# Sixteen-head attention: value products in two groups of six key tiles, and heads packed through memory into one block

## The reference, cut to what matters

```
x1 = layernorm(x)
qh, kh, vh = split(x1 @ Wq.T + bq), split(ctx @ Wk.T + bk), split(ctx @ Wv.T + bv)     # 16 heads of 8
attn = softmax(mask(qh @ kh.T / sqrt(8)))                                              # 56 x 1500 per head
x = x + concat_heads(attn @ vh) @ Wo.T + bo
```

## Time and profile before

| | us |
|---|---|
| median of 3 runs | 3760.95 (3756.37 to 3769.27) |
| the profiled execution | 3759.2 |
| its span | 3757.5 |
| stage L1a, start of its first to its last scores product | 392.8 to 1194.5 |
| stage L2a, the same | 1431.9 to 2231.7 |
| one batch of either in the middle | 25.3 |

### The profile page before, as it was taken

How to read it: one execution, slowest core, us unless ns; L and a number is a source line. 1 busy time by engine, 2 the same in 40 slices (tenths; PEclk the granted TensorE clock), 3 DMA queues, 4 the chain that set the end, 5 groups by cost and what they waited for, 6 DMA issues and landing times. The chain is left out here.

```text
span 3757.5 us, 96452 instructions
## 1 busy us (share of the span) xinstructions
PE 3297.9 (88%) x40550; PEld 2418.8 (64%) x40550; DVE 2546.4 (68%) x3627; ACT 2068.1 (55%) x3846; POOL 1158.9 (31%) x1140
## 2 busy tenths in 40 slices
PE   7676899999998669999999993689999999999989
PEld 4465677777776556777777762456666666666655
DVE  5744677777774447777777746588878787878851
ACT  3321566666564124666656544467676767677733
POOL 0024222212211442222222200145454555555530
PEclk8887999999999788999999996799999999999989
DMA  7954565566562335544554510100000000000000
GB/s 220 267 140 137 155 172 152 155 168 164 143 168 53 99 111 137 137 118 123 138 123 118 137 33 0 32 25 17 25 17 25 24 19 25 17 25 17 17 16 12
DMA packets 136406, 345.99 MB, mean 92 GB/s; under 512 B 56515, under 2 KB 78603, under 8 KB 135979
## 3 DMA queue, kind: packets, MB, share of 16 engines
q1 hardware_dynamic: 132843, 333.40, 33.7%
q0 software_dynamic: 3136, 6.46, 0.5%
HBM read 174.68 MB, written 17.17 MB: 51 GB/s over the span
## 5 line engine op out<-in xcount | busy, mean ns | idle before, releaser
L2115 POOL TENSOR_TENSOR l_S<-l_S,l_shift 125x448 f32<-125x448 f32 (+1 forms) x416 | 461.2, 1151 | 319.9 <-ACT l_shift L2347 317.4
L1431 ACT ACTIVATE L1a_probs<-ps 125x448 f32<-125x448 f32 x768 | 382.7, 545 | 205.7 <-PE ps L1331 192.3
L1431 ACT ACTIVATE L2a_probs<-ps 125x448 f32<-125x448 f32 x768 | 382.8, 544 | 204.9 <-PE ps L1331 191.3
L1464 DVE TENSOR_REDUCE L2a_chunk_max<-ps 112x1 f32<-112x1000 f32 x256 | 301.2, 1197 | 151.0 <-PE ps L1290 150.6
L1464 DVE TENSOR_REDUCE L1a_chunk_max<-ps 112x1 f32<-112x1000 f32 x256 | 301.1, 1196 | 138.5 <-PE ps L1290 138.1
L2328 ACT ACTIVATE ctx_stats<-ps 125x512 f32<-125x512 f32 (+1 forms) x416 | 247.9, 596 | 179.6 <-PE ps L2173 170.4
L2225 PE MATMUL ps<-l_S,l_z 125*128 125x448 f32 x768 | 342.5, 542 | 0.0
L2392 DVE TENSOR_REDUCE l_norms<-ctx_stats 125x8 f32<-125x512 f32 (+1 forms) x416 | 268.3, 676 | 76.9 <-ACT ctx_stats L2328 76.8
L1290 PE MATMUL ps<-L2a_keys,L2a_queries 96*112 96x500 f32 x768 | 264.1, 426 | 47.3 <-DVE L2a_chunk_max L1464 20.3
L2418 DVE SCALAR_TENSOR_TENSOR l_S<-ps,l_neg_cols,l_inv_norms 125x448 f32<-125x448 f32 x384 | 255.4, 679 | 73.6 <-PE ps L2194 69.8
L1235 POOL TENSOR_TENSOR L1a_k_lo<-L1a_k_full,L1a_k_hi 128x1000 fp32r<-128x1000 f32 x64 | 115.0, 1797 | 616.0 <-ACT L1a_k_hi L1388 613.6
(11 more groups left out here) (491 smaller groups left out, 7030.8 us busy)
## 6 DMA issues: line engine op xcount, KB each, us to landing
L1a_keys<-L1a_k_hi SPq DMA_DIRECT2D x256, 187.5 KB
L2a_keys<-L2a_k_hi SPq DMA_DIRECT2D x256, 187.5 KB
a_ctx_T<-in_ctx_T SPq DMA_DIRECT2D x32, 750.0 KB, 12.1
L1a_ctx_T<-in_ctx_T SPq DMA_DIRECT2D x32, 750.0 KB, 6.2
xn<-L_valid SPq DMA_DIRECT2D x32, 750.0 KB, 7.7
L1a_keys<-L1a_k_lo SPq DMA_DIRECT2D x128, 187.5 KB
L2a_ctx_T<-in_ctx_T SPq DMA_DIRECT2D x32, 750.0 KB, 6.4
L2a_keys<-L2a_k_lo SPq DMA_DIRECT2D x128, 187.5 KB
```

The lines of the kernel that those rows point to most:

```text
L1431: nc.scalar.activation(probs[t % NPR][:, h * HQ // 2:(h + 1) * HQ // 2], s.ps[0:KP, i % 3, 0:HQ // 2], ACT.Exp).then_inc(probs_made, 1)
L1464: ins = nc.vector.tensor_reduce(chunk_max[:, n, 0:1], product, AX.XY, ALU.max)
L2115: nc.gpsimd.tensor_tensor(S[b % 2][0:r, t, :], S[b % 2][0:r, t, :], shift[0:r, :], ALU.add)\
```

## The change

- `GT` is 6 instead of 3: the value products come in two groups of six tiles (192 passes each), behind the scores of tile 7 and ahead of the next batch's scores. `NPR` is 10 instead of 6, and the buffers are counted on through the batches.
- The normalized heads go to one of two small tiles, `normed_heads`. SyncE stores each batch's four strips of 8 partitions to memory (`store_heads`), at the end of its turn for the next batch, and loads whole chunks back as one dense block of 128 rows (`load_heads`): three chunks during batches 11, 20 and 29, the rest at the end. `heads_out` is [128, 1792].
- The projection is one product a chunk instead of four, the bias product one instead of four; `wo` and `bv` are loaded dense, without the zeroing of `wo_quad`.
- Queries, their parts and the squares lie in the space of the probabilities; ACT waits once for the stores of the query terms before the batches, DVE no longer does.

```diff
--- before
+++ after
     def bias_product(self, pe):
-        for g in range(4):
-            mm = self.nc.tensor.matmul(self.s.ps[:, 7, 0:1], self.wo_quad[:, g, :], self.bv_quad[:, g:g + 1], start=(g == 0),
-                                       stop=(g == 3))
-        mm.then_inc(self.bias_made, 1)
+        self.nc.tensor.matmul(self.s.ps[:, 7, 0:1], self.wo[:, :], self.bv[:, :], start=True, stop=True)\
+            .then_inc(self.bias_made, 1)
...
-        for g in range(4):
-            mm = self.nc.tensor.matmul(self.s.ps[:, self.CHUNK_BANKS[c], 0:cols.stop - cols.start], self.wo_quad[:, g, :],
-                                       self.heads_out[:, g, cols], start=(g == 0), stop=(g == 3))
-        mm.then_inc(self.projected, 1)
+        self.nc.tensor.matmul(self.s.ps[:, self.CHUNK_BANKS[c], 0:cols.stop - cols.start], self.wo[:, :],
+                              self.heads_out[:, cols], start=True, stop=True).then_inc(self.projected, 1)
...
-    NQ, NKB, NPR, GT = 3, 3, 6, 3
+    NQ, NKB, NPR, GT = 3, 3, 10, 6
...
+    LOAD_AT = [-(-c * 4 * D // SQ) + 1 for c in (1, 2, 3)]
...
+        heads_dram = nc.dram_tensor(f"{layer}_heads", [4, DK, 4, TOK], F32, kind="Internal").ap()
...
-        probs = [sb(f"probs{n}", [KP, HQ]) for n in range(NPR)]
+        probs_space = sb("probs", [D, NPR, HQ])
+        probs = [probs_space[0:KP, n, :] for n in range(NPR)]
+        normed_heads = [sb(f"normed_heads{u}", [D, 4, SQ]) for u in range(2)]
...
-        q, q_hi, q_lo = heads_out[:, 0, :], heads_out[:, 1, :].bitcast(F32R), heads_out[:, 2, :].bitcast(F32R)
+        q, q_hi, q_lo, squares = (probs_space[:, 2 * n:2 * n + 2, :].rearrange("p n c -> p (n c)") for n in range(4))
+        q_hi, q_lo = q_hi.bitcast(F32R), q_lo.bitcast(F32R)
...
-            for j in range(4):
-                sp.dma_start(wo_quad[32 * j:32 * j + DK, :, :], a[f"{layer}_WoT"][j]).then_inc(quads_loaded, 16)
-                if biased:
-                    sp.dma_start(bv_quad[32 * j:32 * j + DK, :], a[f"{layer}_bv"][j]).then_inc(quads_loaded, 16)
+            sp.dma_start(wo[:, :], a[f"{layer}_WoT"].rearrange("j d c o -> (j d c) o")).then_inc(out_loaded, 16)
+            if biased:
+                sp.dma_start(bv[:, :], a[f"{layer}_bv"].rearrange("j d (c o) -> (j d c) o", o=1)).then_inc(out_loaded, 16)
...
-            nc.gpsimd.memset(wo_quad[:, :, :], 0.0).then_inc(zeroed, 1)
...
+            def store_heads(b):
+                sp.wait_ge(normed, b + 1)
+                for j in range(4):
+                    sp.dma_start(heads_dram[j, :, :, b * SQ:(b + 1) * SQ],
+                                 normed_heads[b % 2][32 * j:32 * j + DK, :, :]).then_inc(heads_stored[b % 2], 16)
+
+            def load_heads(first, last):
+                stored = -(-last // SQ)
+                sp.wait_ge(heads_stored[0], 64 * ((stored + 1) // 2))
+                sp.wait_ge(heads_stored[1], 64 * (stored // 2))
+                sp.dma_start(heads_out[:, first:last], heads_dram[:, :, :, first:last].rearrange("j d c q -> (j d c) q"))\
+                    .then_inc(heads_loaded, 16)
...
                 if b + 1 < B:
                     move_maxima(b + 1)
+                if b in LOAD_AT:
+                    load_heads(LOAD_AT.index(b) * 4 * D, (LOAD_AT.index(b) + 1) * 4 * D)
+                if b:
+                    store_heads(b - 1)
+            load_heads(12 * D, (B - 1) * SQ)
+            store_heads(B - 1)
+            load_heads((B - 1) * SQ, TOK)
+            sp.wait_ge(heads_loaded, 16 * 5)
...
-                                          probs[t % NPR][:, h * SQ:(h + 1) * SQ], start=(t == 0 and c == 0),
+                                          probs[(b * KT + t) % NPR][:, h * SQ:(h + 1) * SQ], start=(t == 0 and c == 0),
...
+            act.wait_ge(terms_stored, 96)
...
-                        nc.scalar.activation(probs[t % NPR][:, h * HQ // 2:(h + 1) * HQ // 2], s.ps[0:KP, i % 3, 0:HQ // 2],
-                                             ACT.Exp).then_inc(probs_made, 1)
+                        nc.scalar.activation(probs[(b * KT + t) % NPR][:, h * HQ // 2:(h + 1) * HQ // 2],
+                                             s.ps[0:KP, i % 3, 0:HQ // 2], ACT.Exp).then_inc(probs_made, 1)
...
-                if b == 0:
-                    dve.wait_ge(terms_stored, 96)
...
-                nc.vector.tensor_tensor(heads_out[:, :, b * SQ:(b + 1) * SQ], acc[:, :].rearrange("p (c q) -> p c q", c=4),
+                if b >= 2:
+                    dve.wait_ge(heads_stored[b % 2], 64 * (b // 2))
+                nc.vector.tensor_tensor(normed_heads[b % 2][:, :, :], acc[:, :].rearrange("p (c q) -> p c q", c=4),
...
-            (("heads_out", [D, 4, TOK]), ("wo_quad", [D, 4, D]), ("bv_quad", [D, 4]), ("out_bias", [D, 1])))
+            (("heads_out", [D, TOK]), ("wo", [D, D]), ("bv", [D, 1]), ("out_bias", [D, 1])))
```

More of the change, by code:

```diff
@@ L109, with __init__ @@
     CHUNK_BANKS = (5, 6, 7, 5)
-    def __init__(self, nc, s, stack, name, heads_out, wo_quad, bv_quad, bias):
+    def __init__(self, nc, s, stack, name, heads_out, wo, bv, bias):
         self.nc, self.s, self.stack = nc, s, stack
-        self.heads_out, self.wo_quad, self.bv_quad, self.bias = heads_out, wo_quad, bv_quad, bias
+        self.heads_out, self.wo, self.bv, self.bias = heads_out, wo, bv, bias
         self.sems = [stack.enter_context(nc.semaphore(f"{name}_{n}"))
@@ L1047, in sem @@
             return sems[-1]
-        heads_out, wo_quad, bv_quad, bias = s.heads_out, s.wo_quad, s.bv_quad, s.out_bias
+        heads_out, wo, bv, bias = s.heads_out, s.wo, s.bv, s.out_bias
         wq, wk, wv = sb("wq", [D, D]), sb("wk", [D, D]), sb("wv", [D, D])
@@ L1069, in attention_16_heads @@
         max_hi, max_lo = sb("max_hi", [RT, 2, RW], F32R), sb("max_lo", [RT, 2, RW], F32R)
-        probs = [sb(f"probs{n}", [KP, HQ]) for n in range(NPR)]
+        probs_space = sb("probs", [D, NPR, HQ])
+        probs = [probs_space[0:KP, n, :] for n in range(NPR)]
+        normed_heads = [sb(f"normed_heads{u}", [D, 4, SQ]) for u in range(2)]
         acc, inv = sb("acc", [D, 4 * SQ]), sb("inv", [D, 4 * SQ])
-        q, q_hi, q_lo = heads_out[:, 0, :], heads_out[:, 1, :].bitcast(F32R), heads_out[:, 2, :].bitcast(F32R)
+        q, q_hi, q_lo, squares = (probs_space[:, 2 * n:2 * n + 2, :].rearrange("p n c -> p (n c)") for n in range(4))
+        q_hi, q_lo = q_hi.bitcast(F32R), q_lo.bitcast(F32R)
         if masked:
-            mask_i, valid_all = k_full[0:B, :].bitcast(I32), heads_out[0:B, 3, 0:SK]
+            mask_i, valid_all = k_full[0:B, :].bitcast(I32), squares[0:B, 0:SK]
             neg_all = [k_hi[0:B, :], k_lo[0:B, :]]
@@ L1084, in attention_16_heads @@
             sem(n) for n in ("k_hi_made", "k_lo_made", "queries_made", "max_made", "hi_split", "row_moved", "scores_made"))
[L1085 to L1088, removed]
+        probs_made, probs_used, acc_taken, normed, heads_loaded = (
+            sem(n) for n in ("probs_made", "probs_used", "acc_taken", "normed", "heads_loaded"))
+        heads_stored = [sem(f"heads_stored{u}") for u in range(2)]
+        weights_loaded, mask_loaded, out_loaded, zeroed, cut, prep, q_product, q_made, q_split = (
+            sem(n) for n in ("weights_loaded", "mask_loaded", "out_loaded", "zeroed", "cut", "prep", "q_product",
                              "q_made", "q_split"))
@@ L1103, in load_first @@
                     .then_inc(ctx_loaded[b], 16)
-            sp.wait_ge(zeroed, 6)
+            sp.wait_ge(zeroed, 5)
             if biased:
@@ L1119, in set_first @@
             nc.gpsimd.memset(head_mask[:, :], 1.0).then_inc(zeroed, 1)
-            pool.wait_ge(zeroed, 6)
+            pool.wait_ge(zeroed, 5)
             nc.gpsimd.affine_select(out=head_mask[:, :], in_=head_mask[:, :], compare_op=ALU.is_ge, fill=0.0,
@@ L1134, in set_first @@
             nc.gpsimd.memset(keys[1][KQ:KS, :, :].bitcast(F32), 1.0).then_inc(ones_set, 1)
-        norm(on_sync=load_first, on_pool=set_first, squares=heads_out[:, 3, :])
+        norm(on_sync=load_first, on_pool=set_first, squares=squares)
         batches = ExitStack()
@@ L1541, in _ @@
             norm(("sums", B - 1, 0))
-            dve.wait_ge(quads_loaded, 16 * N_QUADS)
+            dve.wait_ge(out_loaded, 16 * N_OUT)
         batches.close()
         s.stale.append((sems, sem_stack))
-    return Projection(nc, s, ExitStack(), f"{layer}p", heads_out, wo_quad, bv_quad, bias[:, 0:1])
+    return Projection(nc, s, ExitStack(), f"{layer}p", heads_out, wo, bv, bias[:, 0:1])
 def quantized(nc, s, a, norm):
```

6 lines of the change are left out of this document (3 added, 3 removed).

## The result

On one chip, in turns: before 3758.69 us (3756.37 to 3769.27), after 3982.93 us (3979.9 to 3988.22). The ratio is **1.0595, 95% interval 1.0575 to 1.0614**: slower by 224 us. The forecast was 3940 us (3810 to 4005). The profiled execution took 3984.3 us, its span is 3982.6.

The account below looks back on a forecast made before the run. The prediction took TensorE (PE) to set the pace, busy 23.9 of 25.2 us a batch. Its terms, 2 - 7 + 166 + 34 - 19 + 10 - 0.5, less 4 us of existing stalls, gave +181: 3759 + 181 = 3940 us (3810 to 4005).

Parts of the forecast that it names:

- Part 2: Value groups of six in both 16-head stages: TensorE outruns its instruction fetch, 1.3 us a group, +166 us.
- the positions: Page starts relative to a group of six: 128 of 256 give 2.2 us stops, 57 sparse ones part of it.
- Rival 1: Groups of six: instruction fetch keeps up, groups run through, -15 us, 3744 us; chance 11%.
- rival 2: Groups of six: fetch counts from its packet only, 2.4 us; 0.5 us a group, 64 us, 3815 us; chance 10%.
- Part 3: 16-head stages: 38 full stalls each bring a half-clock stretch at 0.9 us, +34 us (0 to 77).
- Part 1: Batch schedule, four groups of three become two of six: +0.03 us a batch, +2 us (-36 to +12).
- first half of the batch: Part 1's step to the next scores behind the first group of six: gain 0.07 us, DVE's chain eats the rest.
- the second half: Part 1's step: second keys product waits for DVE's bank; second group ends at 723.15 against 723.10 before.
- The row of maxima: 16-head stages: the copy of the maxima leaves 0.7 us earlier, so its 14.7 us of waits shrink, -7 us (0 to -15).
- Part 4: Output projection behind each stage: lead of the next layer norm falls from 18.5 to 8.9 us, -19 us for both.
- Part 5: Heads through memory: 0 inside the stage (to +9), 4.9 us bare trip at each stage's end, +10 us for both.

Follow-up runs that it names:

- the twins: phase_few and phase_many: changed kernel with filler instructions making a batch 1024 instructions, differing only in fillers ahead of the first batch; 3929.71 and 4094.91 us.
- half: Changed kernel with each value product taking two heads' columns, so groups of six have 96 passes (half the values wrong); 3760.03 us, 1.0000 of the kernel before.
- run 256: Not a follow-up run and has no measured time: "run" is a verb here, PE executing 256 instructions, one 16 KB packet.
- gt3: Changed kernel with groups of three tiles instead of six, all else of the change kept; 3780.13 us, 1.0015 of the kernel before.
- before_gt2: Kernel before with groups of two tiles and nothing else of the change; 3746.07 us, 0.9939 of the kernel before.
- phase_many: Changed kernel, batches filled to 1024 instructions, 20 and 188 fillers ahead to put page boundaries where stops were long; 4094.91 us, 1.0861 of the kernel before.
- phase_few: Changed kernel, batches filled to 1024 instructions, 92 and 212 fillers ahead to put page boundaries where stops were fewest; 3929.71 us, 1.0410 of the kernel before.
- one_store: Changed kernel with groups of three and one 128-partition store of heads a batch instead of four small ones; 3761.42 us, 1.0005 of the kernel before.

## Why the prediction was right, and where it wasn't

- **Part 2, fetch stops**: +166 forecast; measured 159 us inside the groups and 11.5 just behind them, 1.3 us a group as forecast. Right in cause (the twins, half, the remainder 193) and in size. As many groups stop as the positions gave, 92 of 128 or 72%, like (128 + 57)/256, but not as reckoned: 57 of the 64 second groups and 35 of the 64 first. The size owes something to luck, errors that cancelled: most stops are shorter than 2.2 us (median 1.6), while L1a's first groups stop for 2.88 us in the mean behind the mask's transfers, which no term held. One reading of the mechanism was off: that PE, on entering a page, asks for the one after the next. PE goes on 2.2 to 3.0 us behind the start of the packet each time, so this packet brings the next page; the sum, which lets PE run 256 instructions and then wait, is as it should be. And PE stopped not twice in the stages before but in 10 groups. Rival 1 (the fetch keeps up) and rival 2 (64 us) are out. By the Trainium skill (Runtime: NRT & Kernel Launch, Instruction fetch mechanics) the fetch is hidden by the dispatch; this trace doesn't agree, with 159 us of stops in groups that take an instruction every 6.1 ns (2.34 us for 384).
- **Part 3, clock**: 38 slow stretches forecast at 0.9 us, 33 more came, at 1.3 us by the twins: 42 us against 34. Near in size, but the count was a choice that rested on one gap, and the row was misread: the gap of 1.62 us at 1004.54 is not the longest of the masked stage. This one is, and the clock stayed at 1.00 behind it:

```profile
1156.86 0.48 PE L1331 MATMUL ps<-L1a_queries,L1a_keys 100*125 100x224 f32 x2 [2.02 <-DMA L1a_queries<-L1a_max_lo]
```

- **Part 1, schedule**: the step that was mis-sized. +0.03 us a batch forecast, bounds up to +0.2; measured 25.82 against 25.31 us, some +31 us for both stages. The first half of the batch came out as followed through. In the second half, from the scores behind the first group to the product behind the second, 9.38 us were reckoned; it takes 9.63, and before it takes 9.01 in the median batch, where the sample batch of the earlier trace rows, which held the stop of the earlier trace rows, had 9.26. The second keys product, with no group beside it, waits for DVE's bank (17 us a stage at L1289), as part 1 said, but rows 0 behind it takes 0.93 us to the start of the group, where 0.55 was reckoned. The upper bound was too low.
- **The row of maxima**: -7 forecast; its waits (7.5 and 7.2 us) went wholly, but other waits stand before the same products, 5.4 us instead of 0.8, so -10. That nearly all of the 14.7 us were waits below a microsecond was misread: 8 of the 14 waits were longer, 11.1 us together.
- **Part 4, projection**: the lead 18.5 to 9.0 us in L1a and to 9.9 in L2a, against 8.9 forecast, -18 us. Right.
- **Part 5, trip**: 6.3 and 5.9 us at the two ends against 4.9. The four small stores hold SyncE's queue 0.69 us each (2.76 at 1343.54), where I took 0.31 to 0.33 from the loads of the earlier trace rows: the upper end of my own bound. Inside the stage 0 was right for six tiles, where other waits cover the late context, and +9 for three tiles (gt3).

Sum as measured, between the first and the last `sums` of each stage: +148 (stops in groups, 151.6 less 3.6), +12 (stops behind them), +42 (clock), +31 (schedule), -10 (maxima) and +3, a shift only, as 96 passes a stage that stood ahead of the first `sums` now stand behind it: +226 of +224.7. Outside it is +7 (stops in the first batches), -18, +12 and -3, so -2, where +0.5 was measured. That this closes so well is luck in part. Nor can the 11 us more of the beginning and the 13 less of the end be put down to the change: the first scores product comes at 392.8 us before and at 400.0 in before_gt2, with the same code up to there, and from the first L2258 to the end it is 1250.8 us before and 1236.95 in before_gt2 (1236.65 in the changed kernel). The forecast was 43 us low, 29 us of that the schedule and 8 the clock.

## What to carry to other kernels

Count instructions as well as columns: a run of small products that issues more than a page of 256 instructions in less than the time a page takes to come (here a page entered to the next one usable took 3.7 us in the median stop) stops the engine, whatever the data do; cut such runs, or make each product larger. The stop can also fall just behind the run, on a product that has no part in it. Before lengthening groups to save switches, look at who waits behind a group: here the best group was shorter than the one in use. And an engine that stands still now and then loses twice, as its clock follows.

## What the runs showed of the hardware that was not expected

- **When the packet starts.** A stop ends 2.2 to 3.0 us behind the start of its packet, in all 314 stops inside groups of three kernels (the changed one and the phase twins). But the packet starts between 0.0 and 10.2 us behind the page's first instruction (median 1.1 in the changed kernel). With the boundary between the first and the second group, 60 sparse instructions in 9 us, the packet often came only as the second group began: at 447.94 the page is entered, at 456.26 the packet starts, and the group from 456.19 on stops for 1.0 us. What asks for it so late is open.
- **Stops and clock.** Of the stops inside groups in the changed kernel, 1 of 48 under 1.6 us had a slow stretch at or within 5 us behind it, and 24 of 44 longer ones; in phase_many 10 of 47 and 34 of 76. In phase_few, with 99 stops of which 92 were under 1.6 us, 3 had one. Slow stretches came behind stops that fell just behind a group too, as at 1664.56.
- **Small stores** of eight partitions to memory hold SyncE's queue 0.65 us in the median, the one store of 128 partitions 0.59 (one_store), loads of eight partitions 0.31. Their access patterns differ as well, and what sets the price isn't tested.
